# Two sums of the gradient-magnitude root taken from VectorE into TensorE's PSUM, with smaller feed-forward rings

## The chip, the cores and the metric

One core of one Trainium2 chip. The metric is the device time of one execution in microseconds. Three runs of the kernel before took 1441.74, 1443.97 and 1448.01 us; their median is 1443.97 us. The profile is of one more execution, which took 1447.17 us and has a span of 1445.4 us.

## What is computed

The reference takes 16 images of 3 x 256 x 256 and does three things:

```python
Ix, Iy = depthwise_conv(x, sobel_x), depthwise_conv(x, sobel_y)      # 3 channels
h = sum over channels of hypot(Ix, Iy)                               # 16 x 256 x 256, rows are tokens
h = concat([cls_tok, h])                                             # 257 tokens of 256
h = h + attn(layernorm(h))     # 27 queries, those of the largest norm; 16 heads; the others get the mean
h = h + ffn(layernorm(h))      # 8-bit x ternary linear 256->1024, depthwise conv of 3 taps along the
                               # tokens, silu, 8-bit x ternary linear 1024->256
```

The choice of the 27 tokens and the rounding to 8 bits make small errors in `hypot` visible, so the kernel works the root out beyond what one fp32 operation gives: it splits numbers into a coarse part of few bits and a rest and adds the products one by one.

## The kernel before, in words

**Tiling.** The 16 images are four groups of four. In a group each of the 128 partitions holds 8 image rows (4 images x 32 blocks), and a row with its 3 channels is a tile of 128x768 fp32. The rows are worked in four pairs, i = 0 to 3; `F` in the code are the two rows of a pair. In the text they are the first to the fourth pair.

**Overlap of the groups.** The magnitudes of group g (VectorE, with squares and reciprocal roots on ScalarE) are computed while attention and feed-forward of group g-1 run on TensorE and ScalarE. That is three passes, g = 1, 2, 3. Each engine has its own instruction list, written out in program order; `slot(k)` in the functions called `hypotenuse` is the place between two steps where work of group g-1 is put in. There is no scheduler: what stands ahead of an instruction in its engine's list has to be done first.

**A pair's gradients.** VectorE writes partial rows (`back_parts`, `front_parts`, `edge_row`), and GpSimd adds them by accumulating DMAs (`carried_sums`, three rounds for the x gradient, the rows `nrows_mem`, `img`, `front`). ScalarE then takes absolute values (L1362 for y, L1366 for x) and counts the semaphore `mags`. VectorE waits for it, L614 `max`.

**A pair's hypotenuse**, each step for both rows: max, min; L611 `hi` cuts the larger gradient `mx` to a coarse part `mh`, L614 subtracts it to get the rest `ml`; quotient in int16; products with `mh` and `ml`; ScalarE squares (L1399, `hisq`), VectorE's argument (`arg`), ScalarE's reciprocal root (L1405, `halfrecip`), VectorE's `sh16` (the root in fp16), ScalarE's square (L1410), a correction with its square (L1415, `rstepsq`, which waits for `root_rest`), then VectorE adds up coarse root + step + correction and multiplies by `mx` into `h9` and `others`.

**Feed-forward of group g-1.** 32 tiles per group, i = 8 x image + t. TensorE computes G(i) at L1824 (256->128 channels for 257 tokens) into a PSUM bank; ScalarE copies it to `gpad` (L1461, "s" in the table FFN_SLOTS); TensorE convolves it with three diagonal matrices (L1809), which stands in its list right behind G(i+3); ScalarE adds the bias and stores it in `ydw` (L1464, "t"). After 8 tiles ScalarE runs `silu` (L1447, "a"), 128x2048. The table says in which slot of the third and fourth pair each ScalarE step stands:

```python
FFN_SLOTS = (
    {2: "s0 s1 s2 s3", 3: "t0 s4 t1 s5 t2 s6", 4: "t3 s7", 6: "t4 s8 t5 s9 t6 s10", 7: "t7 s11 a0", 8: "t8 s12 t9"},
    {1: "s13 t10 s14 t11 s15 t12 s16 t13 s17 t14 s18 t15 a1", 3: "t16 s19 t17 s20 t18 s21 t19 s22",
     6: "t20 s23 t21 s24 t22 s25",
     7: "t23 a2 s26 t24 s27 t25 s28 t26 s29 t27 s30 t28 s31 t29 t30 t31 a3"})
```

G has a ring of 4 banks and the convolution another of 4, so TensorE can run up to 4 tiles ahead of ScalarE's takes. After the fourth pair VectorE takes the maxima of the hidden values (L984), image by image; the last needs a3.

**Ends of a pass.** After the feed-forward VectorE normalizes the tokens of group g and selects the 27 (L1053 to L1070), then starts the first pair of the next pass. ScalarE at that place first copies the transposed tokens (L1531), then keys and values of one image (L1550, L1558), and only then takes the absolute values of the first pair (L1362, L1366).

## Time and profile before

| | |
|---|---|
| median of 3 runs | 1443.97 us (1441.74 to 1448.01) |
| profiled execution | 1447.17 us, span 1445.4 us |
| VectorE busy | 1279.4 us, 89% of the span |
| TensorE busy | 805.6 us, 56% |
| ScalarE busy | 739.5 us, 51% |
| GpSimd busy | 202.6 us, 14% |

The page gives shares over the whole span. The chain that ended last is 44% VectorE, 14% TensorE, 10% ScalarE and 10% DMA, so the engine with 89% is not the one bound everywhere: the timelines of the single stretches, with the idle time and its releaser in brackets, show where it is and where it is not.

### The profile page before, as it was taken

Reading aid. Unit: us, or ns where it says so; the run is one execution under the profiler, and the core shown is the slowest. Engines: PE = TensorE matmul, PEld = TensorE weight load, DVE = VectorE, ACT = ScalarE, POOL = GpSimd, SP = SyncE. Lnnn points to the kernel's source line nnn. Section 1 sums busy time; section 2 is a strip of 40 time slices with the busy share of each in tenths; the row PEclk is TensorE's granted clock in tenths of the full one; section 3 lists DMA queues with packets and bytes.
Section 4 is the critical chain, followed back from the end, with each engine's and each line's share of the span. In section 5 each row is a group of like instructions: output and inputs, shape, how many; then the busy total and the mean of one; then the engine's idle time right before and its main releaser. Section 6 shows DMA issues by size and latency. Waiting matters only on the chain.

```text
span 1445.4 us, 11062 instructions
## 1 busy us (share of the span) xinstructions
PE 805.6 (56%) x3316; PEld 636.9 (44%) x3316; DVE 1279.4 (89%) x1962; ACT 739.5 (51%) x1319; POOL 202.6 (14%) x244
## 2 busy tenths in 40 slices
PE   3573400257648764357648773356648774389664
PEld 1341200146437553245536563245536563267553
DVE  7999999899999989989999989989999998812586
ACT  2212324257486764257476765247476864233682
POOL 0011002003213113003223113003222110000000
PEclk8876755677779886577768885567768886587676
DMA  8001504319446518118455617208364410100001
GB/s 215 1 15 15 114 11 78 53 22 164 73 77 103 109 27 142 36 20 152 74 91 91 121 15 140 50 8 132 49 104 79 67 15 30 30 0 1 0 1 29
DMA packets 56367, 92.31 MB, mean 64 GB/s; under 512 B 8643, under 2 KB 37491, under 8 KB 55795
## 3 DMA queue, kind: packets, MB, share of 16 engines
q0 software_dynamic: 41664, 64.50, 27.3%
q1 hardware_dynamic: 14066, 26.31, 7.7%
q10 hardware_dynamic: 576, 0.79, 0.3%
q8 instruction: 26, 0.43, 0.1%
q14 instruction: 35, 0.28, 0.1%
HBM read 22.84 MB, written 4.25 MB: 19 GB/s over the span
## 4 chain that ended last, share of the span: by engine, by line
DVE 44%; PE 14%; DMA 10%; ACT 10%; issue 6%; POOL 0%; DVEq 0%; ACTq 0%
DVE arena L614 16%; DVE arena L617 14%; DMA arena<-nrows_mem 4%; DMA arena<-img 3%; PE psum L1809 2%; DVE arena L984 2%; ACT arena L1447 2%; PE psum L1824 2%; PE psum L1936 2%; DMA arena<-h 2%; DMA arena<-zT 2%; ACT arena L1307 2%; DVE red L630 1%; DVE arena L611 1%; DVE arena L1098 1%
## 5 line engine op out<-in xcount | busy, mean ns | idle before, releaser
L614 DVE TENSOR_TENSOR arena<-arena 128x768 f32<-128x768 f32 (+2 forms) x496 | 455.4, 968 | 13.0 <-ACT arena L1366 11.6
L617 DVE SCALAR_TENSOR_TENSOR arena<-arena 128x768 f32<-128x768 f32 (+2 forms) x224 | 201.5, 949 | 0.1
L1824 PE MATMUL psum<-zT,w1q 128*128 128x257 f32 x512 | 141.9, 417 | 11.0 <-ACT zT L1619 7.3
L1824 PEld LDWEIGHTS psum<-zT,w1q 128*128 128x128 f32 x512 | 107.6, 211 | 31.6 <-issue 8.8
L1809 PE MATMUL psum<-gpad,win 128*128 128x257 f32 x288 | 86.7, 445 | 35.3 <-ACT gpad L1461 35.2
L590 POOL DMA_DIRECT2D h<-others x60 | 51.5, 859 | 384.0 <-DVE others L617 304.8
L1399 ACT ACTIVATE arena<-arena 128x768 f32<-128x768 int16 x32 | 27.0, 844 | 136.3 <-DVE arena L617 135.9
L1809 PEld LDWEIGHTS psum<-gpad,win 128*128 128x128 f32 x288 | 63.6, 225 | 51.2 <-ACT gpad L1461 38.9
L984 DVE TENSOR_REDUCE arena<-arena 128x288 f32<-128x2304 f32 (+1 forms) x17 | 65.2, 3867 | 11.3 <-ACT arena L1448 11.1
L1307 ACT ACTIVATE arena<-arena 128x256 f32<-128x256 f32 x65 | 23.5, 410 | 95.3 <-DVE arena L617 67.0
L1809 PE MATMUL psum<-gpad,onehotT 128*128 128x257 f32 x216 | 56.5, 405 | 23.5 <-ACT gpad L1461 23.5
L617 DVE SCALAR_TENSOR_TENSOR arena<-img 128x768 f32<-128x768 f32 x65 | 59.4, 950 | 8.6 <-DMA img<-x 8.5
L1464 ACT ACTIVATE xT<-psum,cb 128x257 f32<-128x257 f32 x96 | 45.6, 475 | 38.6 <-PE psum L1809 38.6
L1958 PE MATMUL psum<-arena 128*128 128x257 f32 x112 | 45.3, 574 | 33.3 <-issue 27.1
L547 POOL DMA_DIRECT2D arena<-nrows_mem x18 | 15.7, 876 | 319.0 <-ACT arena L1335 247.2
L617 DVE SCALAR_TENSOR_TENSOR arena<-arena,others 128x768 f32<-128x768 int16 x64 | 58.2, 950 | 0.0
L1809 PEld LDWEIGHTS psum<-gpad,onehotT 128*128 128x128 f32 x216 | 43.6, 205 | 32.8 <-ACT gpad L1461 25.9
L1756 PE MATMUL psum<-img,cst 128*128 128x512 f32 (+1 forms) x28 | 16.0, 713 | 73.8 <-DVE arena L617 73.8
L1875 PE MATMUL psum<-cst,arena 128*128 128x128 f32 x64 | 14.7, 392 | 73.2 <-DVE e L614 70.8
L1447 ACT ACTIVATE arena<-xT 128x2048 f32<-128x2048 f32 x14 | 55.2, 3946 | 0.2
L617 DVE SCALAR_TENSOR_TENSOR arena<-arena,small 128x256 f32<-128x256 f32 x131 | 53.3, 480 | 0.6
L1415 ACT ACTIVATE arena<-arena 128x768 f32<-128x768 int16 x32 | 26.9, 844 | 49.2 <-DVE arena L614 48.9
(259 smaller groups left out, 2118.0 us busy)
## 6 DMA issues: line engine op xcount, KB each, us to landing
arena<-img POOLq DMA_DIRECT2D x42, 384.0 KB, 7.6
arena<-nrows_mem POOLq DMA_DIRECT2D x42, 384.0 KB, 8.3
img<-x SPq DMA_DIRECT2D x84, 129.0 KB, 4.0
arena<-arena POOLq DMA_DIRECT2D x21, 384.0 KB, 8.4
h<-others POOLq DMA_DIRECT2D x60, 128.0 KB, 2.7
arena<-zT POOLq DMA_DIRECT2D x12, 384.0 KB, 8.6
out<-out SPq DMA_DIRECT2D x16, 256.0 KB
img<-x SPq DMA_DIRECT2D x48, 64.5 KB, 4.4
```

The source lines that it names most:

```text
L590: pool.dma_start(h9[:, row, :], others[:, row % 2, c, :], accum_op=ALU.add).then_inc(row_sums, 16)
L614: return v.tensor_tensor(o, a, b, op)
L617: return v.scalar_tensor_tensor(out=o, in0=a, scalar=s, in1=b, op0=op0, op1=op1)
L984: return v.tensor_reduce(room.rearrange("p j o r -> p j (o r)"), f4[:, tiles, :, b:b + 1, :].rearrange("p t j o r -> p j (o r) t"), AX, AL ...
L1307: ins = s.activation(ln[1][:, j, :], src(j), ACT.Square)
L1399: s.activation(hsq, short(q), ACT.Square).then_inc(hisq, 1)
L1447: s.activation(fb[:, :, 0:ROWS, :], yd[:, :, 1:S].rearrange("p t (r j) -> p t j r", j=ROWS), ACT.Silu)
L1464: s.activation(ydw[:, t, :], (C0, C1, T0, T1)[i % 4][:, 0:S], ACT.Identity, bias=cb[:, t:t + 1]).then_inc(conv_taken, 1)
L1809: ins = mm((C0, C1, T0, T1)[i % 4][:, 0:S], diagonal(t, k), gpad[:, i % 4, k:k + S], start=(k == 0), stop=(k == 2))
L1824: ins = mm(bank[:, 0:S], w1q[:, k, t * P:(t + 1) * P], zT[:, k, b, :], start=(k == 0), stop=(k == DT - 1))
L1936: ins = mm(C0[:, t * P:(t + 1) * P], y_row(j)[:, t * P:(t + 1) * P], rhs, start=(j == 0), stop=(j == ROWS))
L1958: mm((C0, C1, T0, T1)[hg][:, 0:S], qbd[:, hg // 2, 4 * (hg % 2):4 * (hg % 2) + 4, :].rearrange("p h q -> p (h q)"), keys_of(g, b)[:, hg // ...
```

## The change

In the third and fourth pair of each pass (`SUMMED = (2, 3)`), VectorE no longer makes `mh`, `ml` and the last two additions of the root. ScalarE makes the coarse part, negative, in bf16 (`tops`). TensorE adds `mx` and that coarse part in PSUM by two matmuls with identities, one fp32 and one 16-bit (`rests_of`), and later correction + step + coarse root by three (`roots_of`); step and coarse root are fp16 there. VectorE reads both sums out of PSUM. The two rows' sums lie end to end in the last three banks (C1, T0, T1), so these banks no longer serve the feed-forward: its rings are 3 banks for G and 2 for the convolution instead of 4 and 4, and the transposes of the tokens ahead of it use other banks. In the third pair the edge rows of the next pair stand at slot 1 instead of slot 3. ScalarE's absolute values of a pass's first pair stand ahead of the copies of the transposed tokens. VectorE's counting semaphore runs through a pass, 40 steps for a pair as before and 30 for a summed one.

```diff
+        SUM_BANK = 5
+
+        def sum_parts(f):
+
+            base = SUM_BANK * 512 + f * CH * W
+            return [(psum[:, base + a * W:base + b * W], a, b) for a, b in (((0, 2), (2, CH)), ((1, CH), (0, 1)))[f]]
+
+        def row_sum(f):
+
+            base = SUM_BANK * 512 + f * CH * W
+            return psum[:, base:base + CH * W].rearrange("p (c w) -> p c w", c=CH)
```

VectorE's steps for a summed pair that differ from those of the others (`hypotenuse_summed`), and the edge rows:

```diff
+                    u(stt(t, short(q), 1.0 / GRID, top(mh), ALU.mult, ALU.mult))
...
+                    dve.wait_ge(rests, m2 + 2)
+                    u(stt(ml, short(q), 1.0 / GRID, row_sum(f), ALU.mult, ALU.mult))
...
+                for f in F:
+                    rsq, b, mx, y0, x1, ml, xsq = tmp[f]
+                    dve.wait_ge(rstepsq, n2 + f + 1)
+                    u(tt(rsq, rsq, xsq, ALU.subtract))
+                    u.all()
+                    tt(rsq, rsq, y0, ALU.mult).then_inc(corrections, 1)
+                slot(8)
+                for f in F:
+                    mx = tmp[f][2]
+                    dve.wait_ge(roots, m2 + f + 1)
+                    u(stt(h9[:, bass.ds(2 * i + f, 1), :], row_sum(f)[:, 0:1, :], 1.0 / ROOT, mx[:, 0:1, :], ALU.mult, ALU.mult))
+                    stt(others[:, f], row_sum(f)[:, 1:CH, :], 1.0 / ROOT, mx[:, 1:CH, :], ALU.mult, ALU.mult).then_inc(hypots, 1)
+                dve.wait_ge(hypots, n2 + 2)
...
-                        if k == 3:
+                        if k == (1 if summed else 3):
                             if i == 0:
                                 dve.wait_ge(img_in, g * IMG_IN + IMG_IN)
+                            if summed:
+                                dve.wait_ge(maxima, n2 + 2)
+                                u.all()
                             for f in F:
                                 edge_row(gy_sum(i + 1, f), 2 * i + f + 4).then_inc(carried, 1)
```

ScalarE:

```diff
+                if summed:
+                    for f in F:
+                        mx, mh = tmp[f][2], tmp[f][4]
+                        s.activation(top(mh), mx, ACT.Copy, scale=-1.0).then_inc(tops, 1)
...
-                        s.activation(gpad[:, i % 4, 1:S + 1], (A0, A1, B0, B1)[i % 4][:, 0:S], ACT.Copy).then_inc(gd_ready, 1)
+                        s.activation(gpad[:, i % 4, 1:S + 1], (A0, A1, B0)[i % 3][:, 0:S], ACT.Copy).then_inc(gd_ready, 1)
...
+            gradient_sizes(1, 0)
             tokens_transposed(0)
...
+                if g < GROUPS - 1:
+                    gradient_sizes(g + 1, 0)
                 tokens_transposed(g)
```

TensorE:

```diff
+            def rests_of(g, i):
+
+                n2, m2 = (g * PAIRS + i) * 2, ((g - 1) * len(SUMMED) + SUMMED.index(i)) * 2
+                for f in range(2):
+                    mx, mh = tmp[f][2], tmp[f][4]
+                    pe.wait_ge(maxima, n2 + f + 1)
+                    for dst, a, b in sum_parts(f):
+                        mm(dst, ident, mx[:, a:b, :], start=True, stop=False)
+                        if a == sum_parts(f)[0][1]:
+                            pe.wait_ge(tops, m2 + f + 1)
+                        ins = mm(dst, ident_h[:, :], top(mh)[:, a:b, :], start=False, stop=True)
+                    ins.then_inc(rests, 1)
+
+            def roots_of(g, i):
+
+                n2, m2 = (g * PAIRS + i) * 2, ((g - 1) * len(SUMMED) + SUMMED.index(i)) * 2
+                for f in range(2):
+                    rsq, x1 = tmp[f][0], tmp[f][4]
+                    pe.wait_ge(corrections, m2 + f + 1)
+                    for n, (dst, a, b) in enumerate(sum_parts(f)):
+                        if f == 1 and n == 1:
+                            pe.wait_ge(hypots, n2 + 1)
+                        mm(dst, ident, rsq[:, a:b, :], start=True, stop=False)
+                        mm(dst, ident_h[:, :], half(x1)[:, a:b, :], start=False, stop=False)
+                        ins = mm(dst, ident_h[:, :], sh16[:, f, a:b, :], start=False, stop=True)
+                    ins.then_inc(roots, 1)
+
+            SUM_PLACES = {11: lambda g: roots_of(g, 2), 14: lambda g: rests_of(g, 3), 26: lambda g: roots_of(g, 3)}
+
...
                     if i == 0 or i == 4:
                         pe.wait_ge(diagonals, 2 * g + 1 + i // 4)
                     pe.wait_ge(gd_ready, nt + i + 1)
-                    if i >= 4:
-                        pe.wait_ge(conv_taken, nt + i - 3)
+                    if i >= 2:
+                        pe.wait_ge(conv_taken, nt + i - 1)
                     for k in range(3):
-                        ins = mm((C0, C1, T0, T1)[i % 4][:, 0:S], diagonal(t, k), gpad[:, i % 4, k:k + S],
+                        ins = mm((B1, C0)[i % 2][:, 0:S], diagonal(t, k), gpad[:, i % 4, k:k + S],
                                  start=(k == 0), stop=(k == 2))
                     ins.then_inc(conv_psum, 1)
 
...
                 for b in range(GB):
                     for t in range(FT):
                         i = b * FT + t
-                        if convolve and i >= 4:
-                            pe.wait_ge(gd_ready, g * (GB * FT) + i - 3)
+                        if convolve and i >= 3:
+                            pe.wait_ge(gd_ready, g * (GB * FT) + i - 2)
                         if not convolve and i >= RING:
                             pe.wait_ge(tile_done, i - RING + 1)
-                        bank = (A0, A1, B0, B1)[i % 4] if convolve else banks[i % RING]
+                        bank = (A0, A1, B0)[i % 3] if convolve else banks[i % RING]
                         for k in range(DT):
                             ins = mm(bank[:, 0:S], w1q[:, k, t * P:(t + 1) * P], zT[:, k, b, :],
                                      start=(k == 0), stop=(k == DT - 1))
                         ins.then_inc(g_psum, 1)
                         if convolve and i >= 3:
                             convolution(i - 3)
+                        if convolve and i in SUM_PLACES:
+                            SUM_PLACES[i](g + 1)
...
+                if not last:
+                    pe.wait_ge(idents, 1)
+                    pe.wait_ge(sum2, g + 1)
+                    rests_of(g + 1, 2)
                 for i in range(4):
                     k, t = i // 2, i % 2
                     pe.wait_ge(zs_ready, g * ROW9 + 4 * k + 4)
                     for j in range(4):
-                        ins = tr((T0, T1, B0, B1)[i][:, j * P:(j + 1) * P], zs[:, 4 * k + j, t * P:(t + 1) * P], ident)
+                        ins = tr((A1, B0, B1, C0)[i][:, j * P:(j + 1) * P], zs[:, 4 * k + j, t * P:(t + 1) * P], ident)
```

TensorE's list in the feed-forward, from G(14) on, in the kernel before (psum<-zT,w1q is G, psum<-gpad a convolution, here tiles 11 and 12; brackets name the semaphores waited for):

```order
L1824 MATMUL psum<-zT,w1q 128x257 [waits gd_ready]
L1824 MATMUL psum<-zT,w1q 128x257
L1809 MATMUL psum<-gpad,win 128x257 [waits conv_taken,gd_ready]
L1809 MATMUL psum<-gpad,win 128x257 x2
L1824 MATMUL psum<-zT,w1q 128x257 [waits gd_ready]
L1824 MATMUL psum<-zT,w1q 128x257
L1809 MATMUL psum<-gpad,onehotT 128x257 [waits conv_taken,gd_ready]
L1809 MATMUL psum<-gpad,onehotT 128x257 x2
```

and in the changed kernel, from the convolution of tile 11 on:

```order
L1996 MATMUL psum<-gpad,win 128x257 [waits conv_taken,gd_ready]
L1996 MATMUL psum<-gpad,win 128x257 x2
L1963 MATMUL psum<-arena,cst 128x512 [waits maxima]
L1966 MATMUL psum<-arena,ident_h 128x512 [waits tops]
L1963 MATMUL psum<-arena,cst 128x256
L1966 MATMUL psum<-arena,ident_h 128x256
L1963 MATMUL psum<-arena,cst 128x512 [waits maxima]
L1966 MATMUL psum<-arena,ident_h 128x512 [waits tops]
L1963 MATMUL psum<-arena,cst 128x256
L1966 MATMUL psum<-arena,ident_h 128x256
L2011 MATMUL psum<-zT,w1q 128x257 [waits gd_ready]
L2011 MATMUL psum<-zT,w1q 128x257
```

Eight matmuls that wait for the fourth pair's `maxima` and `tops` now stand between the convolution of tile 11 and G(15). Such a block of 12, which waits for `corrections` and `hypots`, stands behind the convolution of tile 8 and of tile 23 (between it and G(27)), and another of eight ahead of the tokens' transposes.

ScalarE's list where one pass ends and the next begins, in the kernel before (xT<-psum are the transposed tokens, psum,bin_col the keys, zT<-zT and the next row the absolute values of y and x):

```order
L1325 ACTIVATE e<-small 128x8 [waits root_in]
L1530 ACTIVATE xT<-clsT 128x4 [waits yT_psum]
L1530 ACTIVATE xT<-clsT 128x4
L1531 ACTIVATE xT<-psum 128x4x128
L1531 ACTIVATE xT<-psum 128x4x128 [waits yT_psum] x3
L1550 ACTIVATE arena<-psum,bin_col 128x257 [waits k_psum] x2
L1558 ACTIVATE arena<-psum 128x512 [waits v_psum]
L1362 ACTIVATE zT<-zT 128x768 [waits gy_sums_0]
L1362 ACTIVATE zT<-zT 128x768 [waits gy_sums_1]
L1366 ACTIVATE arena<-arena 128x768 [waits gx_sums_0]
L1366 ACTIVATE arena<-arena 128x768 [waits gx_sums_1]
L1387 ACTIVATE arena<-arena 128x768 [waits maxima] x2
```

and in the changed kernel:

```order
L1467 ACTIVATE e<-small 128x8 [waits root_in]
L1501 ACTIVATE zT<-zT 128x768 [waits gy_sums_0]
L1501 ACTIVATE zT<-zT 128x768 [waits gy_sums_1]
L1505 ACTIVATE arena<-arena 128x768 [waits gx_sums_0]
L1505 ACTIVATE arena<-arena 128x768 [waits gx_sums_1]
L1683 ACTIVATE xT<-clsT 128x4 [waits yT_psum]
L1683 ACTIVATE xT<-clsT 128x4
L1684 ACTIVATE xT<-psum 128x4x128
L1684 ACTIVATE xT<-psum 128x4x128 [waits yT_psum] x3
L1703 ACTIVATE arena<-psum,bin_col 128x257 [waits k_psum] x2
L1711 ACTIVATE arena<-psum 128x512 [waits v_psum]
L1533 ACTIVATE arena<-arena 128x768 [waits maxima] x2
```

The four absolute values moved ahead of the copies of tokens, keys and values.

## Rows read from the trace of the kernel before

**Rows 1.** The page's costliest groups, VectorE's maxima; idle time and its releaser behind the bar.

```profile
L984 DVE TENSOR_REDUCE arena<-arena 128x288 f32<-128x2304 f32 (+1 forms) x17 | 65.2, 3867 | 11.3 <-ACT arena L1448 11.1
```

**Rows 2.** Chain of waits, first pass, third pair and last maxima: start us, us.

```profile
467.87 8.47 DMA arena<-nrows_mem
...
539.14 4.07 DVE arena L984
```

**Rows 3.** ScalarE's timeline, third and fourth pair: start, us, what [idle before, releaser].

```profile
442.67 1.72 ACT L1399 ACTIVATE arena<-arena 128x768 f32<-128x768 int16 x2 [4.24 <-DVE arena L617]
...
480.39 1.76 ACT L1393 ACTIVATE arena<-arena,cst 128x768 f32<-128x768 f32 x2
...
492.29 4.00 ACT L1447 ACTIVATE arena<-xT 128x2048 f32<-128x2048 f32 x1
...
503.03 1.28 ACT L1405 ACT_TABLE_LOAD   x1
504.36 1.71 ACT L1405 ACTIVATE arena<-arena 128x768 f32<-128x768 f32 x2
...
513.38 1.71 ACT L1415 ACTIVATE arena<-arena 128x768 f32<-128x768 int16 x2 [3.01 <-DVE arena L614]
```

**Rows 4.** TensorE's timeline, fourth pair, first pass.

```profile
474.02 1.03 PE L1824 MATMUL psum<-zT,w1q 128*128 128x257 f32 x4
482.47 2.94 PE L1809 MATMUL psum<-gpad,onehotT 128*128 128x257 f32 x6 [7.42 <-ACT gpad L1461]
...
489.00 1.46 PE L1809 MATMUL psum<-gpad,wout 128*128 128x257 f32 x6
490.30 1.03 PE L1824 MATMUL psum<-zT,w1q 128*128 128x257 f32 x4
491.17 1.46 PE L1809 MATMUL psum<-gpad,win 128*128 128x257 f32 x6
...
499.81 2.41 PE L1809 MATMUL psum<-gpad,win 128*128 128x257 f32 x6 [1.98 <-ACT gpad L1461]
502.02 1.92 PE L1824 MATMUL psum<-zT,w1q 128*128 128x257 f32 x4
```

**Rows 5.** Windows: us, each engine's busy time, granted clock (PEclk), DMA share, GB/s.

```profile
488.00:497.00 9.00, 9.00 (x43) 7.87 (x42) 9.00 (x11) 7.12 (x7) 0.10 (x1) 1.00 0.35 66
...
499.00:504.00 5.00, 4.19 (x12) 3.38 (x13) 5.00 (x7) 3.76 (x10) 0.00 (x0) 0.66 0.00 0
```

**Rows 6.** TensorE's timeline: identity matmuls of 512+256 fp32 columns; then bf16.

```profile
32.28 2.90 PE L1756 MATMUL psum<-img,cst 128*128 128x512 f32 x4 [13.82 <-DVE arena L617]
...
39.45 1.45 PE L1770 MATMUL psum<-img,cst 128*128 128x512 f32 x4
...
569.65 8.23 PE L1858 MATMUL psum<-w2q,arena 128*128 128x256 bf16 x63
```

**Rows 7.** VectorE's timeline: removed kinds of operation, and the argument of the fourth pair.

```profile
414.37 1.02 DVE L611 TENSOR_SCALAR arena<-arena 128x768 int32<-128x768 int32 x2
...
468.15 3.55 DVE L614 TENSOR_TENSOR arena<-arena 128x768 f32<-128x768 f32 x4
...
503.38 1.82 DVE L617 SCALAR_TENSOR_TENSOR arena<-arena 128x768 f32<-128x768 f32 x2
```

**Rows 8.** VectorE's timeline: SBUF operands alone, then with a PSUM operand.

```profile
582.12 13.13 DVE L617 SCALAR_TENSOR_TENSOR arena<-arena,small 128x256 f32<-128x256 f32 x32
...
601.41 3.62 DVE L617 SCALAR_TENSOR_TENSOR out<-psum,small,out 128x256 f32<-128x256 f32 x9
```

**Rows 9.** VectorE's timeline where the passes begin, then ScalarE's at the second.

```profile
288.80 3.56 DVE L614 TENSOR_TENSOR arena<-arena,zT 128x768 f32<-128x768 f32 x4 [0.67 <-ACT arena L1366]
...
616.53 3.56 DVE L614 TENSOR_TENSOR arena<-arena,zT 128x768 f32<-128x768 f32 x4 [3.21 <-ACT arena L1366]
...
944.23 3.56 DVE L614 TENSOR_TENSOR arena<-arena,zT 128x768 f32<-128x768 f32 x4 [3.18 <-ACT arena L1366]
...
602.59 0.30 ACT L1530 ACTIVATE xT<-clsT 128x4 f32<-128x4 f32 x2 [3.67 <-PE psum L1875]
```

More of the change, by code:

```diff
@@ L127, in tower_kernel @@
     CARRIED_STEPS = 40
+    SUMMED = (2, 3)
+    PASS_STEPS = (PAIRS - len(SUMMED)) * CARRIED_STEPS + len(SUMMED) * 30
     NORM_STEPS = 48
@@ L336, in short, with half, top @@
             return a.bitcast(I16)[:, :, 0:W]
+        def half(a):
+            return a.bitcast(F16)[:, :, 0:W]
+        def top(a):
+            return a.bitcast(BF16)[:, :, 0:W]
         def y_row(j):
@@ L383, in tower_kernel @@
         root16 = sem("root16"); root16sq = sem("root16sq")
+        idents = sem("idents"); tops = sem("tops"); rests = sem("rests")
+        corrections = sem("corrections"); roots = sem("roots")
         rstep = sem("rstep"); rstepsq = sem("rstepsq")
@@ L1351, in next_rows_end, with gradient_sizes @@
                 negate(2)
-            def magnitude_rows(g, i, slot, before_root=None):
-                n2 = (g * PAIRS + i) * 2
-                F = range(2)
+            def gradient_sizes(g, i):
                 pairs_done = (g - 1) * PAIRS + i + 1
-                slot(-2)
-                slot(-1)
-                for f in F:
+                for f in range(2):
                     b = gy_sum(i, f)
@@ L1376, in with_carry, with hypotenuse @@
                         negate(2)
-                hypotenuse(n2, with_carry, before_root)
-            def hypotenuse(n2, slot, before_root=None):
+                hypotenuse(n2, with_carry, before_root, i in SUMMED)
+            def hypotenuse(n2, slot, before_root=None, summed=False):
                 F = range(2)
@@ L1398, in hypotenuse @@
                     act.wait_ge(ratio, n2 + f + 1)
-                    s.activation(hsq, short(q), ACT.Square).then_inc(hisq, 1)
+                    s.activation(hsq, short(q), ACT.Square, scale=ROOT / GRID if summed else 1.0).then_inc(hisq, 1)
                 slot(3)
```

133 lines of the change are left out of this document (119 added, 14 removed).

## The prediction

> **What bounds the kernel now.** I read the chain of waits first. VectorE is its largest part, but the end of the feed-forward goes through the other engines: the last maxima start at 539.14 [rows 2], and before them VectorE has stood idle for a3, the last silu. The page has this wait as 11.1 us over the three passes [rows 1], 3.7 each. So in the fourth pair VectorE is ahead, and what sets the end of a pass is when ScalarE finishes a3. ScalarE's list ties a3 to the hypotenuse: L1415 of the fourth pair ends at 515.1, and a3 is done 24.0 us later [rows 2, 3]. I call that end T.
>
> What sets T? In ScalarE's timeline [rows 3] L1405, the reciprocal root, starts at 504.36 behind a table load that began at 503.03, when the takes of slot 3 were over. VectorE's first argument row, half of the two started at 503.38, was ready at 504.3 [rows 7]. So here both come at the same instant: VectorE's lead is worth nothing from this point if ScalarE doesn't come earlier too, and any delay of ScalarE's takes counts in full. The takes wait for TensorE. TensorE's timeline [rows 4] gives the steps: from the starts 489.00, 490.30 and 491.17, a convolution is 1.30 us and a G 0.87 us, at a granted clock of 1.00, the 2.4 GHz level [rows 5]. After only 1.98 us of idle it took 2.41 (2.21 to the next start) and the G behind it 1.7 (1.92 less the overlap), in a window with mean clock 0.66, part of it on the 1.2 GHz level. After 7.42 us of idle the convolution took 2.73.
>
> **The work removed and added.** In six summed pairs VectorE loses two L611 at 0.51 us and six operations at 0.87 (1.02 for two, 3.55 with overlap for four) [rows 7]: 6.2 us a pair, 37 us in all, if each were on the path. The h9 and others products and one product per row now read PSUM. I price that at nothing: 0.40 us each with a PSUM operand against 0.41 without, on 256 columns [rows 8].
>
> The Trainium skill, VectorE: DVE Perf Modes, section on the TRN2 errata, gives a PSUM source 120 fixed cycles against 58 for SBUF, at 0.96 GHz. By that rule, 36 such operations would cost an estimated 2.3 us more. This trace doesn't show it; by rows the term is zero.
>
> ScalarE gains `tops`, two activations of 128x768 at 0.84, as the two squares' 1.72 with overlap [rows 3]. TensorE gains, per row, 768 fp32 columns, 1.29 us at the high clock (1.45 less overlap) and up to 2.7 at the low one, and one (rests) or two (roots) passes of 768 16-bit columns, 0.39 us each (63 of 256 in 8.23) [rows 6], about 0.6 at the low clock. A rests row is 1.7 to 3.3 us, a roots row 2.1 to 4.0.
>
> **Where a pass begins.** VectorE waits 0.67, 3.21 and 3.18 us for L1366, which stands behind keys and values [rows 9]. Moved ahead, these four values (3.1 us) fill the 3.67 us in which ScalarE waits for TensorE's transposes. The DMA sums are long in by then, because the selection's own loads already wait for them. Saved: 7.1 us. If the values took one us longer than that gap, the copies of keys would be late by as much, but those are needed only some us later: still nothing. The bounds are -7.1 and 0.
>
> **Third pair.** The split's four operations are 2.8 us, and the two edge rows (0.87 each) now fill 1.7 of them. What follows there, the token codes, waits for ScalarE's layernorm sums, so only some 0.5 of the rest comes through; the edge rows are gone from slot 3, which is the other 1.7. VectorE is 2.2 us earlier at its partial rows for the fourth pair. `tops` and rests hold up the transposes and the first takes by 2.3 to 2.6 us, but ScalarE had 4.24 us of slack ahead of L1399 [rows 3]; without it they would cost their 2.6. The fourth pair's x sums are a chain of accumulating DMAs of 8.5 us each [rows 2] that starts with these partial rows, so the third pair can pass on no more than the 2.2 us, however early its root is done. ScalarE, with a0, t8, t9 ahead in its list, allows only 1.0 of it. So the fourth pair's L1393 ends at 481.1 instead of 482.1.
>
> **Fourth pair, slot 1.** Before, TensorE had done G(16) and the convolution of tile 12 by 475.1 and stood idle until s13 came; it then had three convolutions and two G until tile 15 [rows 4]. Now it stops behind tile 11's convolution for `tops`. The first comes at 481.9, the second at 482.8. Idle by then for 4 us, TensorE has the low clock: 1.5 us for what is left of the first row, 3.3 for the second, 486.7. Only then come G(15) to G(18) and four convolutions: 4 x 2.17 = 8.7, 495.4. ScalarE's t15 ends 4.9 us later than before, and so does a1, whose silu began at 492.29 [rows 3]. In VectorE's list nothing is behind a1, but the squares `hisq` are.
>
> **Slot 3.** ScalarE: squares until 503.4, then t16. The ring of 2 lets the convolution of tile 18 start only when t16 is taken, 503.85; with four banks it was ready before. Then, in a row, tile 18, G(22), tile 19: TensorE was idle for 3.2 us, more than the 1.98 that brought the low clock before, so 2.6 + 1.7 + 1.5 = 5.8 us, 509.6. With t19, s22 and the table load (0.75 + 1.28) L1405 starts at 511.7, 7.3 us later than 504.36. The argument is there at 504. From here to L1415 VectorE and ScalarE go hand in hand as before: T is 7.3 us late.
>
> **Tail.** From T, VectorE's two operations per row make the first correction at T+1.0. TensorE has waited since about T-2 or longer, so the roots of the first row take 4.0 and end at T+4.9; the second row's last third waits for `hypots` of the first, and all is done at T+7.0. VectorE ends the pair at T+8.1, as before: the four operations saved there are spent on this wait. Then 5 G and 8 convolutions, 14.8 us, t31 0.45, a3 and its row 4.4: T+26.5 instead of T+24.0. The ring of 4 had let TensorE do three G and two convolutions while a2 ran. So 2.5 us more.
>
> **Sum.** 3 x (7.3 + 2.5) - 7.1 = +22.3 us. Against the profiled execution's 1447.17 that is 1469.5; its own time is 3.2 us above the median of the runs, so for the median 1443.97 + 22.3 = 1466.
>
> **Rivals.**
> - *The clock stays up.* All three new stops cost the high clock's price: rests 1.6, slot 3 2.3, roots 1.9 less. 4.0 us a pass remain, 12 - 7.1 = +5, 1449. For it: TensorE's idle stretches are only 3 to 4 us. Against: 1.98 us already sufficed once.
> - *TensorE's stops stay hidden.* If the ring of 2 and the rests fit into ScalarE's slack, T and a3 come 2.2 us earlier with VectorE: -3 x 2.2 - 7.1 = -14, 1430. For it speaks 3.01 us of idle ahead of L1415 and that ScalarE is busy 51% only. Against: the slack in slot 3 is zero. It decides if ScalarE's slot 3 is over within 1 us of 503.03, and I find it 7 us late.
> - *More low clock.* If also the run of G(15) to tile 15 starts low (+2), and `tops` or the rests' start slips by 1 us: 13 us a pass, +32, 1476.
> - *The change doesn't do what it says where a pass begins*, because another wait (the keys, the slots' loads) takes the place of L1366: +29.4, 1473, inside the forecast's range and counted with it.
>
> **Chances and range.** Forecast 0.60, clock stays up 0.14, hidden 0.16, more low clock 0.10. Faster by over 0.5% means below 1436.8, slower above 1451.2, about what a measurement here can tell. Faster 0.16, same 0.14, slower 0.70. The range 1441 to 1475 holds the forecast's own (1456 to 1475) and the clock rival, and leaves out the hidden case and the very end of the slow one.
>
> **What would show it.** VectorE's wait for L1366 at the passes' beginnings gone. TensorE's rests of the fourth pair starting low and ending about 4 us after L1393. In slot 3, ScalarE's takes waiting twice for convolutions of 1.5 to 2.6 us, and VectorE idle ahead of `sh16` by about 7 us, where there was none. T to a3 26 us or more, VectorE's idle ahead of the last maxima 5 to 6 us. I am wrong if VectorE has no idle ahead of `sh16` in the fourth pair, or if a3 comes no later after the pass's start than before.

## The result, and the profile after

| | before | changed |
|---|---|---|
| median | 1443.15 us, 4 runs (1441.74 to 1448.01) | 1457.66 us, 4 runs (1455.27 to 1462.49) |
| ratio | | 1.0099 (95%: 1.006 to 1.0137) |
| profiled execution | 1447.17 us, span 1445.4 | 1455.27 us, span 1453.4 |
| VectorE, TensorE busy | 1279.4, 805.6 us | 1245.2, 839.9 us |

The changed kernel is slower by 14.5 us. Measured again in another session, it was 1462.9 against 1445.4 us: 1.0129 (1.0114 to 1.0143), 17.5 us. The forecast was +22.3. VectorE lost 34.2 us of work (37 forecast) and the kernel became slower.

The page of the changed kernel, groups of instructions with their idle time behind the bar, answers [rows 1]:

```profile
L643 DVE SCALAR_TENSOR_TENSOR others<-arena 128x768 f16<-128x768 f32 (+1 forms) x52 | 42.1, 852 | 24.4 <-ACT arena L1555 24.2
...
L1124 DVE TENSOR_REDUCE arena<-arena 128x288 f32<-128x2304 f32 (+1 forms) x17 | 65.5, 3885 | 18.6 <-ACT arena L1601 18.4
```

VectorE's wait for the fourth pair's reciprocal root (L1555, before L1405) is new, about 8 us a pass, and its wait for a3 grew from 11.1 to 18.4 us, 6.1 a pass. The work that VectorE was spared has become waiting.

VectorE's timeline where the passes begin, against [rows 9]:

```profile
288.58 3.54 DVE L640 TENSOR_TENSOR arena<-arena,zT 128x768 f32<-128x768 f32 x4
...
620.24 3.54 DVE L640 TENSOR_TENSOR arena<-arena,zT 128x768 f32<-128x768 f32 x4
...
951.67 3.54 DVE L640 TENSOR_TENSOR arena<-arena,zT 128x768 f32<-128x768 f32 x4
```

There is no bracket behind them: the waits of 0.67, 3.21 and 3.18 us are gone.

ScalarE's timeline in the fourth pair of the first pass, against [rows 3] (L1539 is L1393 of before, L1543 makes the coarse parts, L1600 is silu, L1614 copies a G into `gpad`, L1617 takes a convolution, L1549 makes the squares, L1555 is L1405, L1566 is L1415):

```profile
476.83 1.76 ACT L1539 ACTIVATE arena<-arena,cst 128x768 f32<-128x768 f32 x2
478.50 1.56 ACT L1543 ACTIVATE arena<-arena 128x768 bf16<-128x768 f32 x2
...
485.30 0.38 ACT L1614 ACTIVATE gpad<-psum 128x257 f32<-128x257 f32 x1 [3.98 <-PE psum L2011]
...
494.83 3.98 ACT L1600 ACTIVATE arena<-xT 128x2048 f32<-128x2048 f32 x1
...
499.26 1.56 ACT L1549 ACTIVATE arena<-arena 128x768 f32<-128x768 int16 x2
500.73 0.46 ACT L1617 ACTIVATE xT<-psum,cb 128x257 f32<-128x257 f32 x1
...
504.24 0.47 ACT L1617 ACTIVATE xT<-psum,cb 128x257 f32<-128x257 f32 x1 [2.14 <-PE psum L1996]
...
506.75 0.47 ACT L1617 ACTIVATE xT<-psum,cb 128x257 f32<-128x257 f32 x1 [1.77 <-PE psum L1996]
...
508.81 1.58 ACT L1555 ACTIVATE arena<-arena 128x768 f32<-128x768 f32 x2
...
517.83 1.71 ACT L1566 ACTIVATE arena<-arena 128x768 f32<-128x768 f16 x2 [2.60 <-DVE arena L640]
```

The reader is to see three things: s15 waits 3.98 us for a G that stands behind the rests; a1 begins 18.0 us after L1539, where it was 11.9; and slot 3 has two takes that wait for convolutions (2.14 and 1.77 us) where there was one of 1.22, so L1555 comes at 508.81 and not at 504.36. TensorE at these places, against [rows 4] (L1963 fp32 and L1966 16-bit of the rests, L1978 to L1980 the roots, L1996 convolution, L2011 G):

```profile
474.24 1.02 PE L1963 MATMUL psum<-arena,cst 128*128 128x512 f32 x2
479.38 0.61 PE L1966 MATMUL psum<-arena,ident_h 128*128 128x512 bf16 x1 [4.12 <-ACT arena L1543]
...
483.83 0.42 PE L1966 MATMUL psum<-arena,ident_h 128*128 128x256 bf16 x1
484.05 1.16 PE L2011 MATMUL psum<-zT,w1q 128*128 128x257 f32 x4
...
501.32 2.87 PE L1996 MATMUL psum<-gpad,win 128*128 128x257 f32 x6 [3.12 <-ACT xT L1617]
503.99 1.43 PE L2011 MATMUL psum<-zT,w1q 128*128 128x257 f32 x4
505.25 1.46 PE L1996 MATMUL psum<-gpad,win 128*128 128x257 f32 x6
...
520.79 1.12 PE L1978 MATMUL psum<-arena,cst 128*128 128x512 f32 x2 [4.17 <-DVE arena L640]
...
526.35 0.27 PE L1980 MATMUL psum<-others,ident_h 128*128 128x256 f16 x1
```

Windows of the changed kernel in the form of [rows 5] (granted clock third from the end):

```profile
479.00:485.00 6.00, 5.62 (x14) 3.38 (x15) 6.00 (x8) 2.33 (x6) 0.86 (x1) 0.56 1.09 213
501.00:507.00 6.00, 5.67 (x19) 4.72 (x20) 1.01 (x2) 2.09 (x7) 0.00 (x0) 0.72 0.00 0
```

The rests ran almost wholly on the 1.2 GHz level (0.56), slot 3's convolution in part (0.72). VectorE in the same stretch and at the end of the pass, against [rows 2, 7]:

```profile
486.59 1.81 DVE L643 SCALAR_TENSOR_TENSOR arena<-arena,psum 128x768 f32<-128x768 int16 x2
...
491.79 1.82 DVE L643 SCALAR_TENSOR_TENSOR arena<-arena 128x768 f32<-128x768 f32 x2
...
509.69 1.83 DVE L643 SCALAR_TENSOR_TENSOR others<-arena 128x768 f16<-128x768 f32 x2 [7.67 <-ACT arena L1555]
...
524.02 0.42 DVE L643 SCALAR_TENSOR_TENSOR h<-psum,arena 128x256 f32<-128x256 f32 x1 [1.36 <-PE psum L1980]
...
526.66 0.42 DVE L643 SCALAR_TENSOR_TENSOR h<-psum,arena 128x256 f32<-128x256 f32 x1 [1.62 <-PE psum L1980]
...
546.12 4.07 DVE L1124 TENSOR_REDUCE arena<-arena 128x288 f32<-128x2304 f32 x1 [6.13 <-ACT arena L1601]
```

The last maxima are 6.98 us later than at [rows 2] in the first pass, 10.67 in the second, 17.09 in the third. But the span is only 8.0 us longer. The missing 9.1 us are in the last group, in which no pass is left and whose instructions the change leaves alone but for the four banks of its transposes.

### The profile page after: what moved, and what is told of

Read it like the earlier page. It is cut to its first block and busy times, and to the rows that moved or that the text cites. A ratio compares the mean times of both kernels' runs of the same rounds, so it can differ in the third digit from the quotient of the medians.

```text
span 1453.4 us, 11387 instructions
## 1 busy us (share of the span) xinstructions
PE 839.9 (58%) x3484; PEld 647.5 (45%) x3484; DVE 1245.2 (86%) x1914; ACT 751.4 (52%) x1332; POOL 202.3 (14%) x244
## 5 line engine op out<-in xcount | busy, mean ns | idle before, releaser
L640 DVE TENSOR_TENSOR arena<-arena 128x768 f32<-128x768 f32 (+3 forms) x472 | 434.8, 973 | 24.1 <-ACT arena L1505 15.0
L643 DVE SCALAR_TENSOR_TENSOR arena<-arena 128x768 f32<-128x768 f32 (+2 forms) x212 | 191.0, 953 | 2.4 <-ACT arena L1549 2.3
L2011 PE MATMUL psum<-zT,w1q 128*128 128x257 f32 x512 | 132.9, 395 | 15.8 <-ACT zT L1772 9.8
L2011 PEld LDWEIGHTS psum<-zT,w1q 128*128 128x128 f32 x512 | 100.2, 199 | 34.2 <-issue 11.2
L1549 ACT ACTIVATE arena<-arena 128x768 f32<-128x768 int16 x32 | 26.6, 841 | 124.0 <-DVE arena L643 123.6
L1617 ACT ACTIVATE xT<-psum,cb 128x257 f32<-128x257 f32 x96 | 45.2, 471 | 71.3 <-PE psum L1996 71.3
L1124 DVE TENSOR_REDUCE arena<-arena 128x288 f32<-128x2304 f32 (+1 forms) x17 | 65.5, 3885 | 18.6 <-ACT arena L1601 18.4
L1996 PE MATMUL psum<-gpad,win 128*128 128x257 f32 x288 | 74.9, 398 | 9.3 <-ACT xT L1617 9.3
L1996 PEld LDWEIGHTS psum<-gpad,win 128*128 128x128 f32 x288 | 57.1, 199 | 19.3 <-issue 10.5
L643 DVE SCALAR_TENSOR_TENSOR others<-arena 128x768 f16<-128x768 f32 (+1 forms) x52 | 42.1, 852 | 24.4 <-ACT arena L1555 24.2
L1996 PE MATMUL psum<-gpad,onehotT 128*128 128x257 f32 x216 | 53.8, 391 | 14.9 <-ACT xT L1617 14.9
L2064 PE MATMUL psum<-cst,arena 128*128 128x128 f32 x64 | 14.8, 393 | 72.1 <-DVE e L640 69.7
L1600 ACT ACTIVATE arena<-xT 128x2048 f32<-128x2048 f32 x14 | 55.0, 3928 | 0.2
L1996 PEld LDWEIGHTS psum<-gpad,onehotT 128*128 128x128 f32 x216 | 41.2, 193 | 23.1 <-issue 17.2
L2147 PEld LDWEIGHTS psum<-arena 128*128 128x128 f32 x112 | 32.0, 299 | 43.0 <-issue 27.8
```

The lines of the kernel that those rows point to most:

```text
L640: return v.tensor_tensor(o, a, b, op)
L643: return v.scalar_tensor_tensor(out=o, in0=a, scalar=s, in1=b, op0=op0, op1=op1)
L1124: return v.tensor_reduce(room.rearrange("p j o r -> p j (o r)"), f4[:, tiles, :, b:b + 1, :].rearrange("p t j o r -> p j (o r) t"), AX, AL ...
L1549: s.activation(hsq, short(q), ACT.Square, scale=ROOT / GRID if summed else 1.0).then_inc(hisq, 1)
L1600: s.activation(fb[:, :, 0:ROWS, :], yd[:, :, 1:S].rearrange("p t (r j) -> p t j r", j=ROWS), ACT.Silu)
L1617: s.activation(ydw[:, t, :], (B1, C0)[i % 2][:, 0:S], ACT.Identity, bias=cb[:, t:t + 1]).then_inc(conv_taken, 1)
```

## The experiments

One way to read them all is ScalarE's timeline. The table has the mean over the three passes, in us, between the starts of: L1393 of the third and of the fourth pair; the latter and a1's silu; that and the squares; these and the reciprocal root (slot 3); that and L1415; that and a3's silu. The last column is the time from the last maxima of the third pass to the end of the span (the last group). L1393 and L1415 stand for the same steps in every kernel.

| kernel | 3rd to 4th | to a1 | to squares | slot 3 | to L1415 | to a3 | last group |
|---|---|---|---|---|---|---|---|
| before | 55.70 | 11.88 | 5.14 | 6.96 | 9.02 | 21.53 | 250.9 |
| e1_sizes | 55.73 | 11.80 | 5.22 | 7.11 | 9.02 | 21.38 | 247.4 |
| e2_rings | 56.54 | 15.43 | 4.42 | 9.55 | 9.02 | 20.89 | 241.8 |
| e3_third | 54.25 | 15.19 | 4.43 | 9.56 | 9.02 | 21.88 | 241.7 |
| e4_midrings | 54.59 | 17.45 | 4.44 | 5.92 | 9.02 | 24.63 | 250.7 |
| e5_rests4 | 55.03 | 18.35 | 4.43 | 9.55 | 9.02 | 20.88 | 243.1 |
| e6_roots4 | 54.38 | 14.62 | 4.43 | 9.51 | 9.01 | 24.28 | 243.0 |
| changed | 54.29 | 17.41 | 4.43 | 9.94 | 9.02 | 24.67 | 241.8 |
| e8_after_again | 54.72 | 18.25 | 4.43 | 9.55 | 9.01 | 24.52 | 244.6 |
| e9_early_rests | 55.16 | 14.86 | 4.42 | 9.56 | 9.02 | 25.04 | 244.9 |
| e10_place15 | 54.69 | 19.01 | 4.43 | 9.83 | 9.02 | 24.45 | 244.8 |
| e7_freed | 54.06 | 15.20 | 4.44 | 5.91 | 9.02 | 20.58 | 242.7 |
| e11_freed_early | 54.10 | 15.14 | 4.44 | 5.91 | 9.02 | 20.54 | 242.7 |
| e12_before_again | 55.73 | 11.82 | 5.21 | 7.09 | 9.02 | 21.40 | 250.8 |

Ratios are each to runs of the kernel before on the same chip; 0.1% is 1.4 us. The last group's work is the same in all of these kernels, yet it took 241.7 to 250.9 us. What a kernel gained or lost in the passes is therefore also given by its third last maxima, which came at 1194.55 us in the kernel before.

### e1_sizes: the passes' beginnings alone

```diff
+                if g < GROUPS - 1:
+                    gradient_sizes(g + 1, 0)
                 tokens_transposed(g)
```

> The kernel before with one edit: ScalarE's absolute values of a pass's first pair stand ahead of the copies of the transposed tokens. The theory: VectorE's waits of 0.67, 3.21 and 3.18 us for them at the passes' beginnings go and nothing takes their place, so the time is 7 us below the kernel before. The rival (keys and values are late by as much, or the pass meets another wait before its fourth pair): 0 to -2 us.

Measured: 1434.63 against 1443.38 us, ratio 0.9942 (0.992 to 0.9964). In its trace the last maxima of the third pass come 7.03 us earlier than before: the whole of the waits of [rows 9]. The theory stands. What the runs show beyond it (8.7 us) fits the last group, which was 3.5 us shorter here and holds nothing of this edit.

### e2_rings: the short rings alone

```diff
-                        bank = (A0, A1, B0, B1)[i % 4] if convolve else banks[i % RING]
+                        bank = (A0, A1, B0)[i % 3] if convolve else banks[i % RING]
...
-                        ins = mm((C0, C1, T0, T1)[i % 4][:, 0:S], diagonal(t, k), gpad[:, i % 4, k:k + S],
+                        ins = mm((B1, C0)[i % 2][:, 0:S], diagonal(t, k), gpad[:, i % 4, k:k + S],
```

> The kernel before with the feed-forward rings of the changed kernel (3 banks for G, 2 for the convolution, the transposes' banks as there), and VectorE still doing all four sums. Theory A, the rings: in the fourth pair's slot 3 the convolution of tile 18 waits for t16, the reciprocal root comes some 3 us later than 504.36, and the last silu is another 2.5 us later after L1415: 5.5 us a pass, +16 us. Theory B, the sums: what costs is TensorE's rests and roots in its list, the engine has time enough for short rings; the rings alone cost 0 to 3 us.

Measured: 1448.66 against 1443.38 us, ratio 1.0043 (1.0029 to 1.0058). That is +6, between the two theories. The timeline is on the side of A and shows more: the stretch from the fourth L1393 to the reciprocal root is 29.4 us instead of 24.0, 3.5 of it in slot 1 and 2.6 in slot 3, the rest of 0.7 won back in between. The tail doesn't suffer (20.89); A was wrong there. The passes are 12.5 us longer in this trace (the third last maxima come at 1207.03), but the last group is 9 us shorter, and so the time hides most of what the rings cost.

### e3_third: only the third pair summed

```diff
-    SUMMED = (2, 3)
+    SUMMED = (2,)
```

> The changed kernel with only the third pair summed in PSUM (SUMMED = (2,)); the fourth is as before, the rings are 3 and 2 in all of the feed-forward. Theory A, the rings: the fourth pair's slot 3 and the tail still lose 5.5 us a pass, less 1 to 1.5 from the third pair and 7 in all from the passes' beginnings: +16 - 4 - 7 = +5 us against before. Theory B, the sums of the fourth pair: without them the loss is gone, -11 us.

Measured: 1438.26 against 1443.38 us, ratio 0.9963 (0.9947 to 0.9978): 5 us faster, where A expected +5 and B -11. In the trace the passes are 1.8 us longer (third last maxima at 1196.36) and the last group is 9.1 us shorter, so this kernel's lead over the one before is no gain in the passes. The third pair gains 2.3 us a pass against e2_rings (54.25, 56.54), and slots 1 and 3 lose as with the rings alone. Between this kernel and the changed one lies only the fourth pair: some 20 to 24 us by the times, 15.3 and 21.2 us in the passes of the changed kernel's two traces.

### e4_midrings: longer rings in slot 3

```diff
+        G_BANKS[22] = C1
+        C_BANKS[18], C_BANKS[19] = T0, T1
```

> The changed kernel, but the convolutions of tiles 18 and 19 and G of tile 22 use the three banks of the sums, which are free between VectorE's reading of the rests and the roots; so TensorE need not wait for t16 and t17 in the fourth pair's slot 3. Theory A, the rings: the reciprocal root of the fourth pair, now at 508.81, comes 2.7 us earlier and its rest of 1.7 against before comes from a1 behind the rests; -8 us against the changed kernel, so some +6 against before; with what the prediction gave slot 3 alone (all 4.4 of the delay) it would be -13 against the changed kernel. Theory B, the sums: no more than 1 us a pass, the time stays at +13 to +14.

Measured: 1452.29 against 1443.38 us, ratio 1.0066 (1.0041 to 1.0091), 5 to 9 us less than the changed kernel, as theory A had it. (The edit also has the waits that the three banks then need.) In the passes it is 10.0 and 15.9 us less, and the last group took the long 250.7 us. Slot 3 shrank from 9.55 or more to 5.92. TensorE's timeline there, against the 2.87 above:

```profile
500.39 1.57 PE L2019 MATMUL psum<-gpad,win 128*128 128x257 f32 x6 [1.14 <-ACT gpad L1629]
501.80 1.03 PE L2034 MATMUL psum<-zT,w1q 128*128 128x257 f32 x4
```

Tile 18 was done before the slot; tile 19 waited 1.14 us and ran at 1.57, near the high clock's price. So slot 3's delay was the ring of 2 and the low clock behind its wait, 3.6 us and more a pass; slot 1 (17.45) and the tail (24.63) stayed as they were, so the rests' and the roots' prices aren't the rings'.

### e5_rests4 and e6_roots4: the fourth pair's two sums apart

```diff
+    RESTS, ROOTS = (2, 3), (2,)        # e5_rests4
+    RESTS, ROOTS = (2,), (2, 3)        # e6_roots4
```

> The changed kernel, but in the fourth pair only the split's rest comes out of PSUM; the last sum of the root is VectorE's again (its four operations are back, 3 us a pass). The fourth pair's sums cost 20 us in all, by the third-pair kernel at -5.1 and the changed one at +14.5. Theory A, half and half: the rests hold up slot 1 (last take of slot 1 relative to L1393 2.8 us later than without) and the roots hold up the tail (3.4 us more from L1415 to the last silu): this kernel loses some 2 us a pass against the third-pair kernel, about 0 to +2 us against before. Theory B, all from the rests and the low clock behind them: +12 to +14. Theory C, all from the roots: -5.

> The other half: in the fourth pair VectorE makes coarse part and rest itself, and only the root's last sum comes out of PSUM. Theory A, half and half: slot 1 as in the third-pair kernel, the tail 3.4 us longer in each pass, so -5 + 10 = +5 us against before. Theory B, all from the rests: -5. Theory C, all from the roots: +14.

Measured: rests alone 1452.14 us, 1.0052 (1.0041 to 1.0064); roots alone 1449.68 us, 1.0034 (1.0018 to 1.0049), both against 1445.42. Over e3_third (0.9963) that is 0.89% or 13 us for the rests and 0.71% or 10 us for the roots; together 23, as in the changed kernel's second measurement (1.0129). They add up within the intervals. In the passes the two traces are 10.9 and 5.1 us above e3_third's; the roots' traced execution was the fastest of its eight (1446.24 us). The roots came out as theory A has them, the rests at +7 us against before instead of 0 to +2: both halves cost, and the rests more. ScalarE's rows of L1415 and a3, rests alone and then roots alone:

```profile
519.75 1.71 ACT L1618 ACTIVATE arena<-arena 128x768 f32<-128x768 int16 x2 [2.60 <-DVE arena L641]
...
540.72 3.89 ACT L1650 ACTIVATE arena<-xT 128x2048 f32<-128x2048 f32 x1
```

```profile
514.37 1.71 ACT L1616 ACTIVATE arena<-arena 128x768 f32<-128x768 f16 x2 [2.60 <-DVE arena L641]
...
538.45 3.87 ACT L1650 ACTIVATE arena<-xT 128x2048 f32<-128x2048 f32 x1
```

The rests sit in slot 1 (18.35 against 15.19 without), the roots in the tail: 24.08 us in these rows, 20.97 with VectorE's own last additions.

### e7_freed: third pair only, rings of 4 where the banks are free

The edit also has `SUMMED = (2,)` and the waits for the banks.

```diff
+        G_BANKS = [A0, A1, B0, C1, A0, A1, B0, C1, A0, A1, B0, A0, A1, B0, A0]
+        G_BANKS += [(A1, B0, C1, A0)[(i - 15) % 4] for i in range(15, GB * FT)]
+        C_BANKS = [B1, C0, T0, T1, B1, C0, T0, B1, C0, B1, C0, B1, C0, B1]
+        C_BANKS += [(T0, T1, C0, B1)[(i - 14) % 4] for i in range(14, GB * FT)]
```

> The third pair summed alone, and the feed-forward has rings of 4 and 4 again wherever the sums' three banks are free: tiles 3 to 8, and from tile 14 on. Theory A, rings and the fourth pair's sums are the whole loss: the passes' beginnings' 8.7 (as measured) and 1.0 to 1.5 a pass from the third pair: -12 us against before, the fastest. Theory B, the third pair's gain doesn't get past ScalarE's a0 and the fourth pair's gradient sums: -8 to -9, as with the absolute values moved alone. Theory C, the rings were not what cost 5.3 us: -5, as the third-pair kernel.

Measured: 1424.77 against 1445.42 us, ratio 0.9863 (0.9849 to 0.9877). This is the fastest kernel of the study, 1.4% below the kernel before. Theory A expected -12; the runs have -20, and the passes below tell how much of it is A's. ScalarE's timeline in its fourth pair:

```profile
476.92 1.76 ACT L1554 ACTIVATE arena<-arena,cst 128x768 f32<-128x768 f32 x2
...
492.16 4.00 ACT L1615 ACTIVATE arena<-xT 128x2048 f32<-128x2048 f32 x1
...
500.45 0.47 ACT L1632 ACTIVATE xT<-psum,cb 128x257 f32<-128x257 f32 x1 [0.38 <-PE psum L2020]
...
502.51 1.58 ACT L1570 ACTIVATE arena<-arena 128x768 f32<-128x768 f32 x2
```

Slot 1 still pays for the short ring at its start (15.2), but slot 3 is 5.91, a full us below that of before, and a take waits 0.38 us there. The passes are 13.7 us shorter (third last maxima at 1180.83 against 1194.55), 6.6 of it from the beginnings, 4.9 from the third pair (54.06 against 55.70, three times) and 4.1 from the stretch between a pass's start and the third pair, for which no theory here has a reason; the fourth pairs lost 1.9. The last group took 242.7 us instead of 250.9, and that part of the lead is not the change's either.

### e8_after_again and e12_before_again: the same kernels once more

Unchanged kernels, so no diff.

> The changed kernel unchanged, once more, for the spread of its time and a second trace. If the last group's 241.8 us (250.9 in the kernel before) come from TensorE's granted clock of that one execution, this trace may show another value for the same instructions; if it comes from the change, it shows 242 again. Median again 1455 to 1460.

> The kernel before once more, for a second trace: how far the same instructions differ between executions. The last group took 250.9 us in the first trace. If that is TensorE's granted clock of one execution, it may be 241 to 251 here, and the passes within 1 us of the first trace.

Measured: 1462.9 us, 1.0129 (1.0114 to 1.0143), above the expected 1455 to 1460, with a last group of 244.6 us. The kernel before, one execution of 1447.17 us, had 250.8 again and its three passes within 0.3 us of the first trace. So the changed kernel's traces differ (its third last maxima came at 1211.64 and 1217.59, 17.1 and 23.0 us later than before), while the kernel before repeats itself. The short last group is neither that of one lucky execution nor a fixed property of these instructions.

### e9_early_rests: fp32 part of the rests ahead of the wait

```diff
+                for part in sum_parts(0):
+                    larger(0, part)
+                pe.wait_ge(maxima, n2 + 2)
+                larger(1, sum_parts(1)[0])
+                pe.wait_ge(tops, m2 + 1)
```

> The changed kernel, but of each pair's rests TensorE issues the fp32 matmuls with mx as soon as the maxima are there, all but the last 256 columns, and only then waits for the coarse parts. Theory A (what hurts in slot 1 is that TensorE stops for tops with the fp32 work still to do): the rests of the fourth pair, which end at 484.05 in the first pass, end 2 to 2.5 us earlier, a1 with them; the squares hisq are then held by VectorE's ratio instead, which was there by 498.8, so some 1.3 of it goes through to T: 1457 to 1463 becomes 4 us less. Theory B (the time hangs on the number of columns and the low clock alone): within 1 us of the changed kernel.

Measured: 1452.83 against 1443.64 us, ratio 1.0064 (1.005 to 1.0077), 5 to 9 us below the changed kernel. TensorE in the first pass:

```profile
479.68 1.45 PE L1961 MATMUL psum<-arena,cst 128*128 128x256 f32 x4
483.96 0.50 PE L1965 MATMUL psum<-arena,ident_h 128*128 128x512 bf16 x2 [2.83 <-ACT arena L1543]
...
485.05 1.03 PE L2024 MATMUL psum<-zT,w1q 128*128 128x257 f32 x4
```

G comes 1.1 us after the coarse part is there; in the changed kernel it was 4.7 (479.38 to 484.05). Slot 1 falls to 14.86 in the mean, which is no more than without rests (15.19 in e3_third). Theory A, a bit more than it expected by the times: the rests' price in slot 1 goes when the fp32 work stands ahead of the stop. Part of that is the clock. Behind the stop of 2.83 us the granted clock was 1.00 here, where the rests of the changed kernel had 0.56:

```profile
483.90:486.00 2.10, 2.04 (x11) 1.50 (x12) 2.10 (x4) 2.01 (x6) 0.61 (x1) 1.00 1.04 216
```

In the second pass, on the lower level in part, slot 1 was 15.98 us, in the other two 14.30. So some of the gain is the order and some the clock, and the two were not parted further. In the passes the kernel is 1.5 and 7.5 us ahead of the changed kernel's two traces.

### e10_place15: the rests one tile later

```diff
-            SUM_PLACES = {11: lambda g: roots_of(g, 2), 14: lambda g: rests_of(g, 3), 26: lambda g: roots_of(g, 3)}
+            SUM_PLACES = {11: lambda g: roots_of(g, 2), 15: lambda g: rests_of(g, 3), 26: lambda g: roots_of(g, 3)}
```

> The changed kernel with the fourth pair's rests one tile later in TensorE's list, behind G(15) and the convolution of tile 12. Theory A: G(15) runs in the idle time before tops, s15 no longer waits 3.98 us, but the convolution of tile 12 waits for t10 and runs low (2.9 us), so the rests end near 487.5, and three tiles instead of four come behind them: last take of slot 1 within 1 us of before, VectorE waits some 1 us for the rests: time 0 to +3 us against the changed kernel. Theory B (the place is what costs, any tile run ahead of the rests is won): 2 us a pass, -6 us.

Measured: 1464.01 against 1443.64 us, ratio 1.0141 (1.0128 to 1.0154): 2 to 6 us above the changed kernel; its third last maxima come at 1217.59, as in the changed kernel's second trace. The convolution of tile 12 waited 5.56 us for t10 and took 2.91; G(16) followed the rests at 486.21. Slot 1 is 19.0. Theory A: another place in the list doesn't help, the ring ties tile 12 to ScalarE.

### e11_freed_early

The kernel of e7_freed with the order of e9_early_rests.

> The third pair summed alone with rings of 4 and 4 wherever the sums' banks are free (1424.8 so far, -20 against before), with the rests' fp32 matmuls ahead of the wait for the coarse parts. Theory A: rests end 2 us earlier ahead of the tokens' transposes, but the third pair's first takes have slack: 0 to -1.5 us against that kernel, -20 to -22 against before. Theory B (the third pair's start is bound by the transposes behind the rests): -2 a pass, -26 against before.

Measured: 1426.44 against 1443.64 us, ratio 0.9909 (0.9877 to 0.9941). Two of the six executions took 1435.11 and 1440.31 us, the others 1424.7 to 1426.8; why is not known. Its trace has a span of 1423.4 us, that of e7_freed 1423.5. By the traces that is theory A: nothing to be had in the third pair. By the runs it is no faster than e7_freed either, and the two long ones pull its ratio above it.

## Why the prediction was right, and where it was not

**Direction and mechanism: right.** The fourth pair is ScalarE's and TensorE's, and VectorE's savings there turned into waits: 7.67 us ahead of `sh16` (7 forecast), 6.13 ahead of the last maxima (5 to 6 forecast). Three of the rivals fall by the same rows: the clock did not stay up (0.56 over the rests, 2.87 us for the convolution of tile 18), the stops were not hidden (7.67 us), and no other wait took L1366's place (e1_sizes). Of "more low clock" its first part did not come: from G(15) to tile 15 the matmuls ran at 1.03 and 1.46 us, after a G of 1.16.

**The pass.** By the forecast the third pass's last maxima would be 3 x 9.8 - 7.1 = 22.3 us late; the two traces have 17.1 and 23.0. In the second the passes cost what was forecast, in the first they miss it by 5 us of another stretch (below, third pair).

**Where a pass begins: right.** -7.1 forecast, -7.03 in e1_sizes's trace.

**Third pair: right in size, with a wrong split.** L1393 to L1393 is 1.4 and 1.0 us shorter in the two traces (1.0 forecast). It hides a gain of 2.3 from the sums and a loss of 0.8 from the rings, which the prediction didn't have in this pair; with free banks the gain is 1.6. In the first trace the third pass's last maxima are less late by another 5 us that lie ahead of the third pair (by 1 us in the second trace), which no term had. In the second pass 1.3 of its 2.3 us are one wait of VectorE for TensorE's attention (L1936 of before), 0.57 us instead of 1.87. The granted clock over the whole stretch was lower than before (0.70 against 0.75), so it isn't that the clock was higher there on average. The cause stays open.

**Fourth pair, slot 1: the size right, the cause by half.** The forecast's 4.9 us are a difference of absolute times; counted from L1393, which was to come 1.0 earlier, they are 5.9. Measured from L1393 are 5.5 and 6.4. They were put on the rests alone; e2_rings and e5_rests4 part them: 3.5 the ring, which lets TensorE have one tile fewer ready when ScalarE comes, and 3.2 the rests, which are gone when the fp32 matmuls stand ahead of the stop (e9_early_rests). The rests ended 5.5 us after the end of L1393 (484.05 less 478.59); the working has 5.6 there (486.7 less 481.1), and the "about 4" among the signs doesn't fit it. The step "TensorE stops behind tile 11 for `tops`" is right; that the ring of 2 binds already in this slot is what it left out, so that the size fits is in part luck.

**Slot 3: right.** L1393 to the reciprocal root was forecast at 32.3 us (511.7 less 479.4) and is 31.8 and 32.2. The convolution of tile 18 took 2.87 (2.6 forecast), G 1.43 (1.7), tile 19 1.46 (1.5).

**Tail: right to 0.6 us, one cause instead of two.** +2.5 forecast, +3.1 and +3.0 measured from L1415 to a3. It was put on the roots and the ring; e2_rings has no loss in the tail, so it is the roots' alone. The working's own terms give T+26.65 and not 26.5 (7.0 + 14.8 + 0.45 + 4.4); measured in the first pass is T+26.5.

**PSUM operands: right.** Two of 128x768 with a PSUM operand took 1.81 us. Two with the same types and SBUF operands alone took 1.82 in the kernel before:

```profile
491.21 1.82 DVE L617 SCALAR_TENSOR_TENSOR arena<-arena 128x768 f32<-128x768 int16 x2
```

The Trainium skill, VectorE: DVE Perf Modes, section on the TRN2 errata, would have them dearer; this trace does not agree.

**What failed is the step from the passes to the whole**: the prediction added nothing for the last group, since its work is unchanged. It took 9.1 and 6.2 us less than in the kernel before. With that the two traces come out at 17.1 - 9.1 = 8.0 and 23.0 - 6.2 = 16.8 us above the trace of before; the medians, 14.5 and 17.5, are what several executions give, and the execution traced first was the fastest of its four. The last group moved the time away from the forecast both times; the kernel before had the longest of all, twice. The whole last group, before and then changed, in the form of [rows 5]:

```profile
1194.50:1445.40 250.90, 154.09 (x709) 127.40 (x709) 152.75 (x316) 110.84 (x214) 0.00 (x0) 0.70 0.05 13
```

```profile
1211.60:1453.40 241.80, 142.87 (x709) 118.80 (x709) 152.80 (x316) 110.86 (x214) 0.00 (x0) 0.75 0.05 14
```

The same 709 matmuls kept TensorE busy for 154.1 and 142.9 us, and VectorE and ScalarE were busy for the same time in both. The other traces fit in: with a granted clock of 0.70 the group took 250.7 to 250.8 us (e4_midrings, e12_before_again), with 0.72 to 0.73 it took 242.7 to 247.4 (the other eight traces), and with 0.75 it took 241.7 and 241.8 (e3_third, e2_rings). TensorE's rows at one place, before and then changed:

```profile
1278.60 3.65 PE L1936 MATMUL psum<-onehot,arena 128*128 128x128 f32 x16 [2.20 <-DVE arena L1076]
```

```profile
1294.48 2.02 PE L2125 MATMUL psum<-onehot,arena 128*128 128x128 f32 x16 [2.20 <-DVE arena L1216]
```

The same 16 matmuls after the same 2.20 us of idle: 3.65 us at the lower level (granted clock 0.53 over them), 2.02 at the higher (1.00). The windows over that place and the 13 us ahead, before and then changed:

```profile
1262.00:1275.00 13.00, 13.00 (x62) 11.43 (x61) 0.00 (x0) 7.08 (x11) 0.00 (x0) 1.00 0.01 1
1275.00:1287.00 12.00, 9.16 (x60) 8.50 (x58) 2.40 (x4) 2.25 (x6) 0.00 (x0) 0.86 0.01 1
```

```profile
1279.00:1292.00 13.00, 13.00 (x62) 11.34 (x60) 0.00 (x0) 7.51 (x11) 0.00 (x0) 1.00 0.02 2
1292.00:1304.00 12.00, 7.95 (x61) 7.31 (x60) 3.16 (x6) 2.31 (x7) 0.00 (x0) 0.98 0.00 0
```

TensorE was busy without a break ahead of it in both, and the granted clock then was 0.86 and 0.98. What decides it stays open: before, e12_before_again and e4_midrings have 251 us, e1_sizes 247, the others 242 to 245, and neither the rings nor the transposes' banks sort them (e4_midrings has the changed kernel's banks for the transposes and the long time). That this group's difference is TensorE's clock is read from the rows; no run set the clock by itself, and whether the kernels' own timing decides it was not tested.

## What to carry to other kernels

An engine that is busy 89% of the time can still be ahead of the others where the stage ends: before moving its work, look in each stage for the wait that ends last, and move work only where that engine is it (here the third pair, not the fourth). Work given to TensorE in the middle of a ring costs twice, by its stop and by the banks it takes: put the part that needs only early data ahead of the wait, and give the banks back for the stretches in which the sums don't need them (e4_midrings against the changed kernel 5 to 9 us, e7_freed against e3_third 14). Where several traces exist, compare also the stretches that a change leaves alone: they tell how large a difference can come from the clock.
